# Two heads at a time on TensorE: attention's head pairs as 64-row tiles, with scores and maxima in one ring of three PSUM bank pairs

## What is computed

```
x = x + 0.5 * ffn(layernorm(x))
x = x + attn(layernorm(x))
x = x + 0.5 * ffn(layernorm(x))
```

```
scores = einsum('bhsd,bhtd->bhst', q, k) / 8 ** 0.5
scores = where(causal, scores, -inf)
ctx = einsum('bhst,bhtd->bhsd', softmax(scores), v)
return ctx @ wo.T + bo
```

## Time and profile before

| | |
|---|---|
| median of 3 runs | 1189.36 us (1188.13 to 1191.32) |
| span of the profiled execution | 1184.2 us |
| runs' median less that span (launch and end) | 5.2 us |
| attention's matmuls, first maximum to last group | 352.9 to about 937 us |
| first 15 groups | 380.7 to 905.8 us |
| busy share of the span | PE 76%, DVE 54%, PEld 47%, POOL 47%, ACT 41% |

### The profile page before, as it was taken

One profiled execution on the slowest core, in us unless ns is written; L12 is line 12 of the kernel. 1 busy time (PEld: TensorE's weight loads), 2 busy tenths in 40 slices (PEclk: granted clock), 3 DMA queues, 4 the chain that ended last, 5 costly groups with the idle time before them and its releaser, 6 DMA issues. The chain is left out here.

```text
span 1184.2 us, 21961 instructions
## 1 busy us (share of the span) xinstructions
PE 900.6 (76%) x7525; PEld 560.8 (47%) x7525; DVE 636.2 (54%) x1515; ACT 487.1 (41%) x767; POOL 553.3 (47%) x645
## 2 busy tenths in 40 slices
PE   2320899992048999999999799999999622999980
PEld 2320677872023454555555355555554211878770
DVE  6440333331358878878777587787876130333230
ACT  1000343340021676568645477555766301443430
POOL 2775277767510322133427234163323632577776
PEclk9999999997566999999999899999999855999995
DMA  4212676733152114131152302422200113454522
GB/s 146 66 53 84 186 187 158 179 63 28 27 158 47 43 29 149 43 79 45 32 149 67 80 18 58 136 76 63 61 17 13 46 35 113 81 114 69 87 25 19
DMA packets 101649, 92.59 MB, mean 78 GB/s; under 512 B 15348, under 2 KB 80017, under 8 KB 101521
## 3 DMA queue, kind: packets, MB, share of 16 engines
q1 hardware_dynamic: 73024, 71.71, 21.8%
q0 software_dynamic: 27136, 17.09, 10.1%
q10 hardware_dynamic: 1392, 2.51, 0.7%
HBM read 48.32 MB, written 47.12 MB: 81 GB/s over the span
## 5 line engine op out<-in xcount | busy, mean ns | idle before, releaser
L1235 DVE TENSOR_REDUCE m_units<-banks 128x2 f32<-128x512 f32 (+1 forms) x576 | 381.1, 688 | 94.3 <-PE banks L954 78.6
L1184 ACT ACTIVATE pt<-banks 128x1024 f32<-128x1024 f32 (+3 forms) x384 | 291.4, 809 | 163.3 <-PE banks L937 161.4
L954 PE MATMUL banks<-kp,qa 128*128 128x256 bf16 (+1 forms) x1536 | 229.3, 254 | 17.7 <-DMA kp<-k_stack 10.3
L1444 POOL TENSOR_SCALAR_AFFINE_SELECT pt<-pt 128x512 f32<-128x512 f32 x128 | 81.6, 638 | 256.9 <-ACT pt L1184 256.7
L937 PE MATMUL banks<-qb,kp 128*128 128x512 bf16 (+3 forms) x768 | 188.6, 329 | 7.2 <-issue 5.1
L954 PEld LDWEIGHTS banks<-kp,qa 128*128 128x128 bf16 x1536 | 119.5, 99 | 148.7 <-DVE m_units L1235 59.5
L983 PE MATMUL banks<-pt,vs 128*32 128x256 f32 (+2 forms) x2560 | 178.5, 371 | 6.1 <-POOL pt L1444 6.0
L648 ACT ACTIVATE hT<-banks,bfc 128x512 f32<-128x512 f32 (+1 forms) x192 | 113.8, 615 | 168.4 <-DVE bfc L666 94.3
L722 POOL DMA_INDIRECT mid<-ys,ids x80 | 124.9, 1561 | 70.2 <-issue 34.4
L342 POOL DMA_INDIRECT bucket<-rows,row_ix x128 | 125.7, 982 | 64.2 <-issue 38.2
L722 POOL DMA_INDIRECT out_dram<-ys,ids x80 | 123.7, 1546 | 67.8 <-DVE ys L691 32.8
(11 more groups left out here) (166 smaller groups left out, 643.1 us busy)
## 6 DMA issues: line engine op xcount, KB each, us to landing
bucket<-zero SPq DMA_DIRECT2D x16, 660.0 KB, 4.2
xb<-bucket SPq DMA_DIRECT2D x16, 660.0 KB, 4.7
q_stack<-qp SPq DMA_DIRECT2D x24, 256.0 KB, 3.0
k_stack<-kq SPq DMA_DIRECT2D x24, 256.0 KB, 3.7
qa<-q_stack SPq DMA_DIRECT2D x32, 192.0 KB, 3.5
kp<-k_stack SPq DMA_DIRECT2D x32, 192.0 KB, 4.4
qb<-q_stack SPq DMA_DIRECT2D x32, 192.0 KB, 3.4
wfc<-in_L_ffn_c_fc_dram SPq DMA_DIRECT2D x16, 256.0 KB, 3.0
```

The lines of the kernel that those rows point to most:

```text
L954: i = nc.tensor.matmul(a_bank[a % 2][:, j * w:(j + 1) * w], qa[par][:, h, qt * P:(qt + 1) * P], kp[g][:, h // 2, k0:k0 + w], start=not dia ...
L1184: nc.scalar.activation(pt[u % PTS][:, 2 * pair:2 * pair + 2, 0:w], two[pair][:, :, 0:w], ACT.Exp, scale=SCALE).then_inc(exp_done[pair], 1)
L1235: nc.vector.tensor_reduce(m_units[:, qt, at, heads[0]:heads[-1] + 1], a_bank[a % 2].rearrange("p (h k) -> p h k", k=w), AX.X, ALU.max).the ...
L1444: nc.gpsimd.affine_select(out=v, in_=v, compare_op=ALU.is_ge, fill=0.0, base=0, pattern=[[0, HS], [1, P]], channel_multiplier=-1).then_inc ...
```

## The change

`qa` and `qb` hold two heads per slice, as `kp` does, 48 (or 51) rows in partitions from 0 and from 64, without zeros between; the fills with zeros go. Every matmul of scores and maxima reads the 64-row half of its head alone, and the two heads of a pair are issued one after the other into the two banks of a pair. Six banks form a ring of three pairs. Scores and maxima use them in turn, in an order worked out ahead (RING), and each use waits for the reader of the use three before. A unit of maxima is now a bank pair with up to 1024 columns: 20 units per group instead of 36, allotted 2, 2, 2, 2, 2, 2, 2, 1, 2, 1, 1, 1 to the units u. The diagonal blocks of a half come together, four to a unit, with the causal mask put into both banks. `values` has one side of up to 512 queries and comes once per unit, after the second score. `m_units` becomes `m_blk` with 10 columns per query tile.

```diff
+    HB = T // 2
+    M_COLS = 10
+    M_DIAG = 6
+    MUNITS = []
     for hf in (1, 0):
+        full = [(qt, [(qt, 0, HB)], qt % HB, 2) for qt in range(HB, T)] if hf else []
+        over = HB * hf
+        ends = [([(over + HB - 1, over, HB - 1)], HB - 1, M_COLS - HB + 1),
+                ([(over + 1, over, 1), (over + 2, over, 2)], 1, M_COLS - 1)]
...
+        for pair in range(2):
+            MUNITS.append((hf, pair, [(HB * hf + j, HB * hf + j, 1) for j in range(HB)], 0, M_DIAG, True))
...
+    M_IN_UNIT = [2, 2, 2, 2, 2, 2, 2, 1, 2, 1, 1, 1]
...
+    RING = []
+    for u in range(NU):
+        ms = list(range(M_FROM[u], M_FROM[u + 1]))
+        RING += [("score", 2 * u)] + [("max", m) for m in ms[:1]] + [("score", 2 * u + 1)] + [("max", m) for m in ms[1:]]
+    SLOT = {use: i % 3 for i, use in enumerate(RING)}
...
-            qa = [sba(f"qa{i}", [P, HS, S], bf16) for i in range(2)]
-            qb = [sba(f"qb{i}", [P, HS, S], bf16) for i in range(2)]
+            qa = [sba(f"qa{i}", [P, HS // 2, S], bf16) for i in range(2)]
+            qb = [sba(f"qb{i}", [P, HS // 2, S], bf16) for i in range(2)]
...
-            a_bank, o_bank, c_bank = bank[4:6], bank[6], bank[7]
+            ring, o_bank, c_bank = two_banks[0:3], bank[6], bank[7]
...
+                def slot_free(entry, n, more, first):
+                    (kind, k), same = slot_before(entry, more)
+                    if not same and first:
+                        pe.wait_ge(m_done, max(m for m in range(NM) if m % 3 == SLOT[entry]) + 1)
+                    elif kind == "score":
+                        wait(pe, e_done, NS * (n if same else n - 1) + k + 1)
+                    else:
+                        wait(pe, m_done, NM * (n + 1 if same else n) + k + 1)
...
                     for s in range(2):
-                        i = nc.tensor.matmul(two[pair][:, s, 0:w], kp[g][:, pair, kb * P:(kb + 1) * P],
-                                             qb[par][:, 2 * pair + s, q0:q0 + w], start=True, stop=True)
-                    i.then_inc(st_full[pair], 1)
+                        rows_s = slice(64 * s, 64 * s + KS + 3)
+                        i = nc.tensor.matmul(ring[SLOT["score", 2 * u + pair]][:, s, 0:w],
+                                             kp[g][rows_s, pair, kb * P:(kb + 1) * P],
+                                             qb[par][rows_s, pair, q0:q0 + w], start=True, stop=True)
+                    i.then_inc(s_full, 1)
...
+                    if diag:
+                        for s in range(2):
+                            nc.tensor.matmul(ring[slot][:, s, :], identb[:], causal[:].rearrange("p h k -> p (h k)"),
                                              start=True, stop=False)
+                    at = 0
+                    for j, (qt, kb, blocks) in enumerate(segs):
+                        for s in range(2):
+                            rows_s = slice(64 * s, 64 * s + KS)
+                            i = nc.tensor.matmul(ring[slot][:, s, at:at + blocks * P],
+                                                 qa[par][rows_s, pair, qt * P:(qt + 1) * P],
+                                                 kp[g][rows_s, pair, kb * P:(kb + blocks) * P],
+                                                 start=not diag, stop=not diag or j == len(segs) - 1)
...
+                        for pair in range(2):
+                            slot_free(("score", 2 * u + pair), n, more, first)
+                            score(par, g, n, u, pair)
+                            if pair == 1:
+                                if u >= LAG:
+                                    values(par, n, u - LAG)
+                                elif not first:
+                                    values(1 - par, n - 1, NU - LAG + u)
+                            if more and m0 + pair < m1:
+                                slot_free(("max", m0 + pair), n, more, first)
+                                maxima(ng, nb, m0 + pair, SLOT["max", m0 + pair])
...
+                for m in range(NM):
+                    wait(pe, m_done, m - 2)
+                    maxima(0, 0, m, m % 3)
+                    if m == NM1 + 2:
+                        max_rows_of(pro_at[("max1", 0)], 0, 1)
...
+                    nc.vector.tensor_reduce(dst, ring[slot][:, :, 0:blocks * P].rearrange("p s (j k) -> p s j k", k=P),
+                                            AX.X, ALU.max).then_inc(m_done, 1)
...
-                nc.vector.memset(qa[0][:], 0.0)
                 norm(0)
-                for t_ in qa[1:] + qb:
-                    i = nc.vector.memset(t_[:], 0.0)
-                i.then_inc(cleared, 1)
```

More of the change, by code:

```diff
@@ L1066, in step @@
                             pe.wait_ge(max_ld[0][par], 32 * uses_of(b, g))
-                        a0, a3 = A_FROM[u], A_FROM[u + 1]
-                        for i in range(4):
-                            if i < 2:
-                                score(par, g, b, n, u, i)
-                            elif u >= LAG:
-                                values(par, n, u - LAG, i - 2)
-                            elif not (bt.first and g == 0):
-                                values(1 - par, n - 1, NU - LAG + u, i - 2)
-                            if more and a0 + i < a3:
-                                maxima(n + 1, ng, nb, a0 + i, a0 + i + 1)
+                        first = bt.first and g == 0
+                        m0, m1 = M_FROM[u], M_FROM[u + 1]
+                        for pair in range(2):
+                            slot_free(("score", 2 * u + pair), n, more, first)
[8 more added lines that the diff above has]
+                                maxima(ng, nb, m0 + pair, SLOT["max", m0 + pair])
                         if u == 1:
@@ L1328, in step @@
                     for u in range(NU):
-                        for a in range(A_FROM[u], A_FROM[u + 1]) if more else ():
-                            reduce(n + 1, a)
-                            if g == 0 and not bt.first and NA1 <= a < NA1 + T:
-                                t = a - NA1
+                        for m in range(M_FROM[u], M_FROM[u + 1]) if more else ():
+                            reduce(n + 1, m, SLOT["max", m])
+                            if g == 0 and not bt.first and NM1 <= m < NM1 + T // 2:
+                                t = 2 * (m - NM1)
                                 if t == 0:
                                     dve.wait_ge(c_evac, at["o_p1"] + 1)
-                                router_sums(x2, t, t + 1)
+                                router_sums(x2, t, t + 2)
                         if u == 2 and ("ctx0", g - 1) in at:
@@ L1382, in _ @@
                 norm_task(pro_at, "v1", 0)
-                for a in range(NA):
-                    reduce(0, a)
+                for m in range(NM):
+                    reduce(0, m, m % 3)
                 sweep(nc.vector, step)
```

146 lines of the change are left out of this document (64 added, 82 removed).

## The result

The changed kernel takes 1204.54 us in the median of four runs (1201.62 to 1212.47); the kernel before, on the same chip, 1190.34 (1188.13 to 1191.91). The ratio is 1.0136 with the interval 1.0099 to 1.0173: 14 us **slower** (1.4%), where 1141 was forecast. The profiled execution is the longest of the four, 1212.47 us with a span of 1210.7, so launch and end are 1.8 us. They are 1.8 us in every listed run of the kernel before too. So of the 5.2 us that were put down to them under "Time and profile before", 3.4 say that the execution profiled there was faster than the median. The two profiles thus lie 26.5 us apart where the medians lie 14 apart: a fast execution of the one kernel stands against the slowest of the other.

A forecast was written before the change was run, and what follows sets the result against it. PE's stream was taken as the bound. Fifteen groups at 474.6 us plus 5.2 for the clock give 479.8 against 525.1 (-45.3); with -3.4 ahead of the sweep, -48.7 from 1189.4: 1141 us, range 1112 to 1174.

The forecast's parts named there:

- The stream and the tiles: Scores and maxima: 64-row tiles overlap fully, saving 7.7 us of PE stream per group; 1024-element reductions take 1.22 us.
- The loop: Full units of the sweep: score, values, maximum and reduction wait on each other through three bank pairs, 3.0 us per unit.
- light groups: Sweep groups with almost nothing beside attention: 29.8 us each, four of them 119.2 us.
- Ahead of the sweep: First maxima before the sweep: fewer, wider reductions end 3.4 us earlier, and the first score follows.
- Group 15: Last group of the sweep, which makes no maxima: stays as it was, its scores waiting for ACT and POOL.
- the loop's turn: Before group 8, PE waits for its own instructions: 5.1 us, kept in the forecast sum.
- The clock: Group 0 and the group after the turn start at 1.2 GHz for two full units: 2.6 us each, 5.2 together.
- The cover: PE's side tasks after a unit's last maximum: about 1.3 us per unit hides them, so projections cost next to nothing.
- rival 4: Row tiles in scores and maxima do not overlap: loop 3.4, light group 34.1 us, about 1200 us in all; chance 0.05.
- Rival 3: Granted clock falls in the sweep: light group grows to 43.2 us, half the groups so give 1241 us; chance 0.08.
- Rival 1: Exchange of the maxima becomes each group's wait: one to two us per group, 1156 to 1171 us; chance 0.18.
- Rival 2: Unit loop is shorter than counted and DVE alone bounds the sweep: 1052 us, halfway 1100; chance 0.08.

The follow-up runs named there:

- e2: Changed kernel with the values of unit u-2 issued ahead of the odd score instead of behind it; 1196.52 us, ratio 1.0063.
- e3: Changed kernel with only the 64-row tiles undone: zeros back in qa and qb, every score and maximum matmul reads 128 rows; 1214.11 us, ratio 1.0206.
- e9: Changed kernel plus zero-weight matmuls where its clock fell: two in units 0, 1, 8, 9, six in the router group's unit 8; 1191.93 us, ratio 1.0011.
- e11: Changed kernel with full 128-row matmuls, values ahead of the odd score, DVE's side tasks behind the next unit's first maximum; 1204.82 us, ratio 1.012.

## Why the prediction was wrong, step by step

**The stream and the tiles: right.** Full overlap (two 512-column matmuls in 0.23 us by the distance of starts), reductions of 1024 elements in 1.22 us and of 768 in 0.95, twenty of them per group:

```profile
L1276 DVE TENSOR_REDUCE m_blk<-banks 128x8 f32<-128x1024 f32 x192 | 231.4, 1221 | 112.9 <-PE banks L989 111.7
L1276 DVE TENSOR_REDUCE m_blk<-banks 128x6 f32<-128x768 f32 x128 | 120.8, 953 | 33.5 <-PE banks L989 32.8
```

**The loop: right.** 3.03 us against 3.0, and 3.46 with full rows against 3.4; light groups 30.0 and 30.3 against 29.8. e2 shows the loop's make-up: with the values outside it, u2 takes 2.6 instead of 3.1.

**Ahead of the sweep: right but small.** 3.4 us were forecast, 4.6 came (1.3 to 4.0 in the experiments on the changed kernel); the first score now waits 2.4 us for the exchange of the maxima, where it had waited 0.46. Group 15 (29.1) and the loop's turn (5.23 against 5.10 us of issue) are unchanged, as said.

**The clock: the step that failed most.** The prediction let the clock be low "for two full units" at two places, some 17 us at 0.50 that cost 5.2 us, and held it at 1.00 elsewhere because group 15 had stood at 1.00 up to 922 us. That row was of a stretch in which PE was busy for 15.12 of 17 us with values in two sides and full-array matmuls. The sweep has 144 us at 0.50. The price that was set down, 1.28 us per loop, was near the 1.17 measured; what was mis-sized is how long the clock is low. It fell after PE had waited (3.51 us in the router's stall), but also with PE's records nearly without a gap: at 602.60, behind a stretch with 3.29 us busy of 3.40, in which stood sixteen router matmuls of 8 columns. A record's length holds the way through the array, so "busy" is not stream.

That the row tiles bring the low clock is shown by e3 (22 us low with full rows in the same ring), and that it costs time by e9. For the price in the changed kernel there are four readings:

- The loop loses 0.28 us per low us.
- Group 6 against group 4, both of the changed kernel, takes 7.50 us against 6.27 for u2 and u3 with 3.4 us low: 0.36.
- From the changed kernel to e9, groups 1, 5 and 9 lose 2.8, 2.1 and 1.8 us for 6.6 low us each (2 × 0.09 × 36.6): 0.34 on average.
- The sweeps of the two differ by 14.2 us, with about 0.9 of fill in 14 groups 27, for 79 low us less (144 to 65): 0.34.

The last two take the fill at its price in group 2; without any price of the fill the sweeps give 0.18. At 0.28 to 0.34, 144 low us cost 40 to 49 us, where 5.2 had been set down: some 38 us of the 72.5 by which the sweep missed (552.3 against 479.8, in the slowest of four executions). This is an estimate; no run held the clock in the changed kernel without adding work.

The Trainium skill (TensorE: Matmul & The Clock Gate, A second HAM failure mode: psum-queue depth-cycling) tells of a kernel that cycles through PSUM banks, whose short idles between groups of matmuls let the clock go back and forth. Here the trace agrees: outside the router's stalls the ring's waits last up to 1.6 us, and the clock is below 1.00 in 13 of the 15 groups. I had weighed only the long wait as its cause and gave the rival 0.08.

**The cover: the second.** "After a unit's last maximum there are 1.43 us ... about 1.3 us per unit is cover" let the projections cost "next to nothing". At full clock (e9 less its fill) those groups take 33.8 to 35.5 against 30.8. The step took one figure, the wait of a full unit, for all twelve, while the side tasks stand in units of other kinds. In group 2 PE is busy for 25.03 of 30.00 us, so by its records there are 5 us of waits in the whole group, 0.4 per unit. Group 5 against group 2, from odd score to odd score at a clock of 1.00, shows where the side tasks were covered:

| from the odd score of | group 2 | group 5 | on PE's queue between them in group 5 |
|---|---|---|---|
| u4 | 2.71 | 2.71 | a transposition, 0.59: covered |
| u5 | 2.67 | 3.58 | a projection, 1.06; the even score and a masked maximum nearly fill the time of the reduction |
| u6 | 3.47 | 3.46 | a projection: covered |
| u7 | 1.46 | 2.75 | a projection, and 0.28 of wait for DVE's part of the last one |
| u8 | 2.45 | 3.28 | PE waits 0.94 for an exponential, behind two side operations of ACT |
| u9 | 1.69 | 2.67 | a projection |
| u10 | 2.26 | 2.64 | PE waits 0.44 for a reduction, behind DVE's part of the last projection |

PE from the odd score of u7 on, group 2 and then group 5:

```profile
469.46 0.23 PE L969 MATMUL banks<-qb,kp 51*128 51x128 bf16 x2 [1.10 <-DVE m_blk L1276]
...
470.92 0.38 PE L969 MATMUL banks<-qb,kp 51*128 51x512 bf16 x2
```

```profile
570.30 0.23 PE L969 MATMUL banks<-qb,kp 51*128 51x128 bf16 x2
...
571.60 1.13 PE L1042 MATMUL banks<-xnT,wkT 128*128 128x512 f32 x2 [0.28 <-DVE rest L1325]
...
573.05 0.38 PE L969 MATMUL banks<-qb,kp 51*128 51x512 bf16 x2
...
574.94 0.34 PE L989 MATMUL banks<-kp,qa 48*128 48x128 bf16 x4 [0.94 <-ACT pt L1218]
```

Units u7 and u9 have one maximum each, and the odd score behind them takes a bank pair that an exponential frees and not a reduction, so the wait that was to hide the projection is not there. Of the 4.4 us that group 5 is longer in these rows, about 2.9 are PE's own work on three projections, 0.8 stand behind ACT's queue and 0.7 behind DVE's. The kernel before paid as much (by the same cut 35.6 for groups 1, 5 and 9 against 31.3 for group 2), so the ring hid nothing more than the old order: the prediction had this case, "if the cover were gone they would cost the 5 us". The waits' list of 377 to 929 us shows how the ring couples the engines:

```profile
DVE m_blk L1276 <- PE banks L989: 133.2, 142, 5.5
...
PE banks L969 <- DVE m_blk L1276: 37.7, 66, 1.1
PE banks L989 <- DVE m_blk L1276: 12.1, 6, 3.5
```

DVE waits for maxima and PE for their reduction, in turn. In the router groups the stop itself was in the sum (3.7 us and 0.2 more); what was not are the router's transpositions and logits on PE in u3 to u5 (9.6 us at a clock of 1.00 in group 6 against 7.9 in group 2). The size of this step: at full clock the six projection and output groups are 1.4 to 4.7 too long, the three router groups 2.2 to 3.0 (41.8 less 0.3 × 17 low us is 36.7 against 33.7), together some 30 us, an estimate again. With the 38 of the clock that is most of the miss of 72.5; the rest, some 5 us, is spread over the light and scatter groups.

**What this leaves of the idea.** The change put two things together. The ring with full rows costs 2.1% (e3), or 1.2% in its best order (e11), with the clock held; the row tiles give back 0.7% and 1.0%. So even at a held clock the ring is a loss that the tiles have to earn back. The prediction had this in rival 4, the ring with tiles that do not overlap, but at about 1200 us, where e3 takes 1214.

**The rivals.** Rival 3 (the clock falls, slower) had the right side, with the mechanism but at the wrong place: it had whole groups low, and what came were some twenty short stretches, most of 3 to 7 us, two of 17. It was 0.08 and should have been the first. Rival 1 (the exchange of maxima) did not come: PE waits for that DMA only once, at the sweep's start (2.4 us). Rival 2 did not: DVE waits 144.5 us for maxima (111.7 and 32.8 in the two rows of the reductions). Rival 4 did not: tiles overlap. Had the clock been held, the sweep would be near 552 - 45 = 507 and the kernel near 1162 (1212.5 - 45 - 5, the last 5 for the last layer of this execution). These are estimates by the price above, and no run shows them; the forecast's 1141 was out of reach even so, for the cover.

## What to carry to other kernels

When a change thins the stream of the engine that bounds, ask two things before counting the gain: which waits of that engine turn from none to many short ones (the granted clock may fall with them, and each low us cost about 0.3 us here), and in which units it still waits once the loop has replaced it. A side task is covered only in a unit where its own engine waits, and for no longer than that wait; look for it unit by unit, and not by one mean. In the other units it costs its full time, and what it leaves in the queue of another engine ahead of a link of the loop costs too (0.3 to 0.9 us each here). Tiled matmuls pay where they stand side by side; one tiled pair between full-array ones saves 0.21 us and pays 0.22.

## What the chip showed that was not expected

Extra work made the kernel faster: the zero-weight matmuls of e9 took 12.6 us off (1204.54 to 1191.93), with 79 us less of the sweep at 1.2 GHz. The clock fell once right behind a stretch of which PE's records cover 3.29 of 3.40 us. And the changed kernel's runs spread over 11 us (1201.62 to 1212.47) where the four runs of the kernel before, taken with them, spread over 4; that the spread comes from where the low stretches fall was not tested.
